# A four-layer graph network on one core: the last sweep over the adjacency matrix with every block split, into nine plus four slots

## The reference

```python
x = _layernorm(x + _L0_gnn_ref(x, adj, W_self, W_neigh))   # adj @ h / deg, deg = clip(row sums of adj, 1)
x = _layernorm(x + _L1_gnn_ref(x, adj, kernel, bias))      # relu(adj @ (x @ K) + bias)
x = _layernorm(x + _L2_gnn_ref(x, adj, W1, b1, W2, b2))    # relu twice: two products with adj
x = _layernorm(x + _L3_gnn_ref(x, adj, W, b))              # x1 = swish(adj @ x @ W + b), x2 = swish(adj @ x1 @ W + b)
```

## Time and profile before

| | |
|---|---|
| median of 3 runs | 1170.21 us (1168.99 to 1171.78) |
| the profiled execution, its own time | 1166.82 us |
| its span, first to last instruction | 1164.6 us |
| PE busy | 1143.0 us, 98% |
| DVE busy | 810.4 us, 70% |
| ACT busy | 539.0 us, 46% |
| granted TensorE clock, mean | 0.996 |
| DMA | 279.45 MB, mean 240 GB/s |

### The profile page before, as it was taken

One profiled execution on the slowest core, in us unless ns is written; L12 is line 12 of the kernel. 1 busy time (PEld: TensorE's weight loads), 2 busy tenths in 40 slices (PEclk: granted clock), 3 DMA queues, 4 the chain that ended last, 5 costly groups with the idle time before them and its releaser, 6 DMA issues.

```text
span 1164.6 us, 13823 instructions
## 1 busy us (share of the span) xinstructions
PE 1143.0 (98%) x4936; PEld 887.7 (76%) x4936; DVE 810.4 (70%) x1091; ACT 539.0 (46%) x612; POOL 69.4 (6%) x48
## 2 busy tenths in 40 slices
PE   7999999999999999999999999999999999999995
PEld 3455767778778888888888888888888888887673
DVE  4888889889898666685545488656496555655883
ACT  1112334444655444474445464544375444544673
POOL 0000000000131111000000010101000000000111
PEclk9999999999999999999999999999999999999998
DMA  8988666655868656496656578566578566756893
GB/s 295 375 290 280 233 226 227 223 203 199 304 238 298 211 192 217 173 339 232 210 189 199 182 268 307 182 216 200 198 276 293 203 204 209 261 219 231 317 337 142
DMA packets 82626, 279.45 MB, mean 240 GB/s; under 512 B 8832, under 2 KB 14208, under 8 KB 82560
## 3 DMA queue, kind: packets, MB, share of 16 engines
q1 hardware_dynamic: 75744, 273.71, 66.9%
q10 hardware_dynamic: 6816, 4.85, 1.4%
HBM read 276.43 MB, written 2.10 MB: 239 GB/s over the span
## 4 chain that ended last, share of the span: by engine, by line
PE 89%; DMA 4%; DVE 3%; ACT 1%; issue 1%; ACTq 1%; POOL 0%; POOLq 0%; DVEq 0%; SPq 0%
PE acc L425 25%; PE acc L420 25%; PE acc L421 25%; PE acc L408 10%; PE acc L457 3%; DMA out<-t_x 2%; DVE adj_lo L685 1%; DMA b<-L_b 1%; DMA raw<-adj_tiles 1%; ACT t_x L526 1%; ACT adj_hi L569 1%; PE acc L443 1%; PE acc L435 1%; DVE stats L600 0%; ACTq L556 0%
## 5 line engine op out<-in xcount | busy, mean ns | idle before, releaser
L685 DVE TENSOR_TENSOR adj_lo<-raw,adj_hi 128x1024 fp32r<-128x1024 f32 x426 | 516.5, 1230 | 210.0 <-ACT adj_hi L569 194.6
L569 ACT CAST adj_hi<-raw 128x1024 fp32r<-128x1024 f32 x426 | 445.2, 1050 | 403.3 <-PE acc L425 243.9
L420 PE MATMUL acc<-adj_hi,op_hi 128*128 128x512 f32 x1352 | 538.4, 398 | 0.0
L421 PE MATMUL acc<-adj_hi,op_lo 128*128 128x512 f32 x1352 | 526.7, 390 | 0.0
L425 PE MATMUL acc<-adj_lo,op_hi 128*128 128x512 f32 x1352 | 417.6, 390 | 1.8 <-DVE adj_lo L685 1.8
L425 PEld LDWEIGHTS acc<-adj_lo,op_hi 128*128 128x128 f32 x1352 | 253.1, 188 | 58.3 <-DVE adj_lo L685 5.4
L420 PEld LDWEIGHTS acc<-adj_hi,op_hi 128*128 128x128 f32 x1352 | 254.1, 188 | 55.2 <-issue 4.3
L421 PEld LDWEIGHTS acc<-adj_hi,op_lo 128*128 128x128 f32 x1352 | 254.1, 188 | 55.0 <-issue 4.3
L589 DVE TENSOR_TENSOR deg_part<-deg_part,raw 128x1024 f32<-128x1024 f32 x120 | 146.6, 1222 | 13.3 <-DMA raw<-adj_tiles 8.3
L408 PE MATMUL acc<-raw,x_rows 128*128 128x512 f32 x312 | 140.7, 600 | 6.8 <-DMA raw<-adj_tiles 6.8
L708 POOL TENSOR_TENSOR rstd<-var_eps,minus_half 128x4 f32<-128x4 f32 x32 | 56.6, 1769 | 1083.2 <-DVE var_eps L605 1083.2
(11 more groups left out here) (45 smaller groups left out, 224.8 us busy)
## 6 DMA issues: line engine op xcount, KB each, us to landing
raw<-adj_tiles SPq DMA_DIRECT2D x518, 512.0 KB, 4.8
x_rows<-x_blocks SPq DMA_DIRECT2D x8, 256.0 KB, 6.2
xt<-x_t ACTq DMA_DIRECT2D x8, 256.0 KB, 5.5
out<-t_x ACTq DMA_DIRECT2D x8, 256.0 KB, 4.2
w<-W ACTq DMA_DIRECT2D x2, 64.0 KB, 8.9
b<-b ACTq DMA_DIRECT2D x2, 64.0 KB, 12.5
w_res<-W_self ACTq DMA_DIRECT2D x1, 64.0 KB, 3.5
w_neigh<-W_neigh ACTq DMA_DIRECT2D x1, 64.0 KB, 4.6
```

The costliest lines, as they stand in the source:

```text
L420: nc.tensor.matmul(bank, op_block(op_hi, p, j), a_hi, start=first and b == 0, stop=False)
L421: nc.tensor.matmul(bank, op_block(op_lo, p, j), a_hi, start=False, stop=False)
L569: nc.scalar.copy(adj_hi[:, s % SPLIT, :], raw[:, g % RAW, :]).then_inc(hi_ready, 1)
L685: nc.vector.tensor_tensor(adj_lo[:, s % SPLIT, :], raw[:, g % RAW, :], adj_hi[:, s % SPLIT, :].bitcast(fp32), ALU.subtract).then_inc(lo_re ...
```

## The change

It does five things.

1. The seven WHOLE blocks of LAST_ORDER become ONE: all 60 steps of the last sweep are split. `kept` and `hidden` go, and the line 408 form with `deg_part`.
2. Four more split slots, numbers 9 to 12, from the load of step 430 on. Slot 9 + i is the quarter i (1024 wide) of `op_hi` and `op_lo` of parity 0, pass 4's operand, from when the last product of pass 4 that reads it is done (COLUMN_END: products 673, 693, 697 and 699).
3. A split step takes the slot whose last reader comes first, instead of slot s % 9. For all steps up to 442 this is the same product to wait for as before. From then on:

| step | waits for product, before | after |
|---|---|---|
| 443 | 674 | 673 |
| 458 | 691 | 690 |
| 459 | 700 | 691 |
| 460 | 701 | 693 |
| 461 | 702 | 697 |
| 462 | (WHOLE) | 699 |
| 463 | (WHOLE) | 700 |
| 464 | 703 | 701 |
| 468 | 707 | 705 |
| 471 | 710 | 708 |
| 512 | 749 | 749 |
| 517 | 754 | 754 |

From 464 on a split may run 13 steps ahead of PE (step g waits for product g + 237).

4. Nearly all entries of the tables move. In passes 0 to 4 most move by one step or one product (WEIGHT_AT by 1, the others by 8 or 16). In the last sweep they move further, as shown:

| chunk m | 40 | 41 | 42 | 43 | 44 | 45 | 46 | 47 |
|---|---|---|---|---|---|---|---|---|
| WEIGHT_AT, before / after | 720/720 | 725/726 | 731/732 | 738/738 | 741/742 | 749/750 | 762/762 | 768/768 |
| SUM_AT, ahead of the split of step | 471/480 | 476/486 | 484/492 | 489/496 | 494/499 | 502/504 | 512/513 | end/end |
| SCALE_AT, ahead of the split of step | 479/489 | 484/494 | 494/498 | 502/502 | 506/505 | 512/end | end/end | end/end |

5. A load waits for the subtraction of the step six before it in all of the last sweep, since no step of it is WHOLE.

```diff
     LAST_ORDER = (
-        [(0, 1, 1, ONE), (0, 2, 1, ONE), (0, 3, 1, WHOLE), (0, 5, 5, ONE), (0, 0, 0, ONE), (0, 5, 6, ONE),
+        [(0, 1, 1, ONE), (0, 2, 1, ONE), (0, 3, 1, ONE), (0, 5, 5, ONE), (0, 0, 0, ONE), (0, 5, 6, ONE),
...
-    KEPT = [CHUNKS - 1 - q for q in (1, 2)]
...
+    COLUMN_END = {k: max(at for at, (g, ahead) in enumerate(PRODUCTS) if STEPS[g][0] + ahead == LAST - 1 and STEPS[g][2] == k)
+                  for k in range(CHUNKS)}
+    SPLIT_SLOT = {}
+    SPLIT_BEFORE = {}
+    slots = [(-1, slot, None) for slot in range(SPLIT)]
+    for s, g in enumerate(SPLIT_STEP):
+        if g == min(step for step in SPLIT_STEP if STEPS[step][0] == LAST):
+            slots += [(max(COLUMN_END[2 * i], COLUMN_END[2 * i + 1]), SPLIT + i, max(COLUMN_END[2 * i], COLUMN_END[2 * i + 1]))
+                      for i in range(4)]
+        until, SPLIT_SLOT[s], SPLIT_BEFORE[s] = min(slots, key=lambda slot: slot[:2])
+        slots.remove((until, SPLIT_SLOT[s], SPLIT_BEFORE[s]))
+        slots.append((LAST_USE[g], SPLIT_SLOT[s], LAST_USE[g]))
...
             def whole_step(at, g, k, h):
                 bank, first, ends = begin(at)
-                if SUM_OF[at][0] == 0:
-                    pe.wait_ge(x_loaded[k], 16)
-                    rows = cols(x_rows, k)
-                else:
-                    pe.wait_ge(op_ready, op_no(LAST, k) + 1)
-                    rows = kept(k)
+                pe.wait_ge(x_loaded[k], 16)
...
+        def split_hi(s):
+            slot = SPLIT_SLOT[s]
+            if slot < SPLIT:
+                return adj_hi[:, slot, :]
+            return op_hi[:, (LAST - 1) % 2, (slot - SPLIT) * TW:(slot - SPLIT + 1) * TW]
...
-                    if s >= SPLIT:
-                        wait_split_used(act, s - SPLIT)
-                    nc.scalar.copy(adj_hi[:, s % SPLIT, :], raw[:, g % RAW, :]).then_inc(hi_ready, 1)
+                    wait_split_free(act, s)
+                    nc.scalar.copy(split_hi(s), raw[:, g % RAW, :]).then_inc(hi_ready, 1)
```

More of the change, by code:

```diff
@@ L329, in rows4, with split_lo @@
             return t.rearrange("p (b d) -> p b d", b=BPC)
-        def kept(k):
-            return deg_part[:, 0, KEPT.index(k) * CW:(KEPT.index(k) + 1) * CW]
-        def hidden(c):
-            return kept(c) if c in KEPT else t_x[:]
+        def split_hi(s):
[3 more added lines that the diff above has]
+            return op_hi[:, (LAST - 1) % 2, (slot - SPLIT) * TW:(slot - SPLIT + 1) * TW]
+        def split_lo(s):
+            slot = SPLIT_SLOT[s]
+            if slot < SPLIT:
+                return adj_lo[:, slot, :]
+            return op_lo[:, (LAST - 1) % 2, (slot - SPLIT) * TW:(slot - SPLIT + 1) * TW]
         def norm_no(m):
@@ L346, in wait_raw, with wait_split_free @@
             eng.wait_ge(raw_loaded[g % RAW], 16 * (g // RAW + 1))
-        def wait_split_used(eng, s):
-            g = SPLIT_STEP[s]
-            if g in EARLY_NO:
-                eng.wait_ge(e_done, EARLY_NO[g] + 1)
-            else:
-                eng.wait_ge(f_done, g + 1)
+        def wait_split_free(eng, s):
+            if SPLIT_BEFORE[s] is not None:
+                g, ahead = PRODUCTS[SPLIT_BEFORE[s]]
+                if ahead:
+                    eng.wait_ge(e_done, EARLY_NO[g] + 1)
+                else:
+                    eng.wait_ge(f_done, g + 1)
         @block.sync
@@ L407, in whole_step @@
                     j = h * BPT + b
-                    last = nc.tensor.matmul(bank, rows[:, j * P:(j + 1) * P], raw[:, g % RAW, b * CW:(b + 1) * CW],
+                    last = nc.tensor.matmul(bank, cols(x_rows, k)[:, j * P:(j + 1) * P], raw[:, g % RAW, b * CW:(b + 1) * CW],
                                             start=first and b == 0, stop=ends and b == BPT - 1)
@@ L424, in split_step @@
                     j = k * BPC + h * BPT + b
-                    last = nc.tensor.matmul(bank, op_block(op_hi, p, j), adj_lo[:, s % SPLIT, b * CW:(b + 1) * CW],
+                    last = nc.tensor.matmul(bank, op_block(op_hi, p, j), split_lo(s)[:, b * CW:(b + 1) * CW],
                                             start=False, stop=ends and b == BPT - 1)
@@ L511, in after @@
                         act.wait_ge(op_ready, m + CHUNKS)
-                    nc.scalar.activation(hidden(c), t_y[:, m % 2, :], ACT.Silu).then_inc(silu_ready, 1)
+                    nc.scalar.activation(t_x[:], t_y[:, m % 2, :], ACT.Silu).then_inc(silu_ready, 1)
                 if p == LAST and u == SILU_AT[m]:
@@ L540, in after @@
                         act.wait_ge(silu_ready, m - 4 * CHUNKS + 1)
-                        nc.scalar.copy(dst, hidden(c)).then_inc(op_hi_ready, 1)
+                        nc.scalar.copy(dst, t_x[:]).then_inc(op_hi_ready, 1)
                 if p == LAST and u == SCALE_AT[m]:
@@ L667, in after @@
                     if p in (0, 4):
[L668 removed]
+                        nc.vector.tensor_tensor(lo, t_x[:], hi, ALU.subtract).then_inc(op_ready, 1)
             for u in range(END * PARTS):
```

46 lines of the change are left out of this document (22 added, 24 removed), and 22 rows, old and new, of tables (BIAS_AT, NORM_AT, SCALE_AT, SUM_AT).

## The result

| | before | after |
|---|---|---|
| median of the runs | 1170.2 us (1168.99 to 1171.78) | 1158.12 us (1157.24 to 1159.29) |
| the profiled execution, its own time | 1166.82 us | 1157.31 us |
| its span | 1164.6 us | 1155.1 us |

The ratio is 0.9895, with an interval of 0.988 to 0.9911. The changed kernel is 12.1 us faster by the medians and 9.5 us by the profiled executions. The prediction had the sign, but 1164.1 us and a range from 1161.0 were too high: it saw 6.1 us of gain.

What follows compares the result with a forecast made beforehand. PE's work and waits were taken as the bound. Terms -4.97 (work), -5.16 (waits), +2.0 (waits back) and +2.05 (tail) sum to -6.1; from the median 1170.2 that forecast 1164.1 us, range 1161 to 1170.5.

Steps and rivals of the forecast that it cites:

- Part 1: Last sweep on PE: fourteen steps split instead of WHOLE, 1.36 us for 1.715 each, giving -4.97 us.
- Part 2: Last sweep, slots and loads: loads run ahead, removing 5.16 us of PE waits, less 2 us that come back.
- dating by hand: Last sweep: event times worked out from profile rows; PE never waits, but four margins are under a microsecond.
- reserve: Last sweep: 2 us of PE waits allowed for slower hand-offs and late stores, range 0 to 5 us.
- better: Last sweep and tail: no waits, and chunk 46's scaling or its store falls into a gap; 1161 to 1162 us, chance 0.10.
- late loads: Last sweep: loads every 1.46 us, sum copies late, PE waits 5 to 9 us; 1167 to 1171, say 1169, chance 0.15.
- lockstep: Last sweep: ACT and DVE wait for each other, 13.5 us per six-step chunk; 12 us slower, 1174 us, chance 0.12.
- Not running ahead: Last sweep: DMA or load slots still hold the loads, saved PE time becomes waits; 1172 us, chance 0.08.
- Part 3: Tail after PE's last work: last scaling waits for chunk 46's store; 14.15 us instead of 12.11, +2.05 us.
- Part 4: Passes 0 to 4: work moves by one step or product, 1.36 to 2.7 us, within 5.6 us of cover; no change.

Runs made afterwards that it cites:

- nine-slot run: Changed kernel without the four extra split slots, its last-sweep tables mostly four steps earlier: 1166.71 us, ratio 0.9977 to the kernel before.
- second pair: Both kernels profiled once more without edits: kernel before 1167.49 us profiled (runs 1168.37), changed kernel 1158.53 us profiled (runs 1158.65, ratio 0.9907).

## Why the prediction was wrong, by its steps

**Part 1 was right.** The work of the last sweep is 87.8 us where it was 92.8; the splits of the fourteen steps cost nothing, for DVE had room (17 of 20 us busy). With 60 products at 1.36 the sweep is down to its nominal work within 0.4 us, and the gain in work is the 4.97 of the rows: the pair of WHOLE products took 3.43 us in the trace, and the 6.4 us of gain would have asked for 3.63.

**Part 2 was right in its mechanism, and its size was off.** The loads run ahead from 1045 us on (291, 297, 360 GB/s), the casts with them, and nothing waits. The dating by hand held. The copies of sums 41 to 44 in ACT's timeline:

```profile
1075.62 0.59 ACT L507 COPY t_agg<-acc 128x512 f32<-128x512 f32 x1 [0.26 <-PE acc L440]
...
1084.95 0.57 ACT L507 COPY t_agg<-acc 128x512 f32<-128x512 f32 x1
...
1093.80 0.59 ACT L507 COPY t_agg<-acc 128x512 f32<-128x512 f32 x1 [0.20 <-PE acc L440]
...
1102.09 0.58 ACT L507 COPY t_agg<-acc 128x512 f32<-128x512 f32 x1
```

They end at 1076.21, 1085.52, 1094.39 and 1102.67. With the 1.63 us by which this execution was early that is 1077.8, 1087.2, 1096.0 and 1104.3, against 1078.0, 1088.1, 1096.1 and 1104.1. The **failed term** of the sum is the one set beside the dating: "2 us of waits, with 0 and 5 as the ends", a reserve for hand-offs and late stores that no row asked for. The waits were 0.38 and 0.26. Where each event is dated from rows and the dates say none, the likeliest value was none. The case called "better" was half true: there were no waits, but the scaling of chunk 46 fell into no gap, and its 1161 to 1162 was still too high. The reserve is only 1.6 of the 6.0 us between 1164.1 and 1158.1; the rest stands under "What is left".

**The late loads did not come**, and the rival had two things wrong. First, it held a load every 1.46 us against PE's 1.36. PE needs a step every 1.36 only up to product 719; from there a multiplication by the weights stands in about every six products, which the prediction itself puts at 9.05 us, 1.51 for a step. From 1060 to 1080 the changed kernel's DMA moved 361 GB/s, which is the rival's rate, and yet the lead was 15.8 us at step 470 and 15.9 at step 490. Second, 359 isn't the most that the loads can bring. The same 20 us of the kernel with the entries of chunks 0 to 39 as before:

```profile
1060.00:1080.00 20.00, 17.29 (x74) 14.21 (x73) 18.13 (x17) 15.92 (x17) 0.00 (x0) 0.91 1.01 403
```

By the Trainium skill (SBUF — State Buffer, "A bandwidth-pool intuition that's wrong", about 358 GB/s to a core) the prediction had the lead lose 2 us in 20 products; in this trace it kept 15 to 18 us up to product 743. The 361 of the changed kernel agrees with that figure, and the 403 lies above it.

**The lockstep** didn't come either, in this kernel. In the nine-slot run ACT and DVE do come late, with 6 us of waits and not 12; that this is the alternation of the two that the rival describes isn't shown. **Not running ahead** can be ruled out by the windows.

**Part 3 was right:** 14.0 us for the forecast 14.15, with the store landing 2.3 us after its issue, as forecast, and the last scaling waiting 2.42 us for it.

**Part 4 was right** in its size. The waits in passes 1 to 4 are the same within half a microsecond, and the run with the entries of chunks 0 to 38 as before is as fast as the changed kernel.

**What is left.** The forecast of the profiled executions was -6.1, and they gave -9.5 and -9.0. Of the 3.4 and 2.9 that are missing, 1.6 to 1.7 are the reserve for waits, 1.6 and 0.4 the start of product 708, and 0.1 to 0.2 the tail; in the second pair the kernel before also waited 0.6 us more. The start of product 708 is luck for the most part: two profiles of one and the same kernel differ in it by 0.1, 1.3 and 2.0 us, in the three kernels profiled twice. The rest of the miss, 2.6 us, is in the base: the median lay 3.4 us above the profiled execution before, and only 0.8 after. The prediction added its difference to the median of three runs, 1170.2; the five other medians of the kernel before were 1168.3 to 1169.4, its 35 timed executions on one chip lie between 1167.1 and 1172.3, and the profiled executions had 1166.8 and 1167.5. So the miss of 6.0 us is made up of 1.6 for the reserve, 0.1 for the tail, 1.6 for the start and 2.6 for the base. With the measured waits in place of the reserve the forecast would have been 1162.5, still outside what came. The range left too little on its lower side: the sum with no waits is 1162.1, and less the 1.4 us by which runs differ 1160.7, above the 1158.1 measured. The timed gain was 10.7 us on a shared chip, 1.5 more than the mean of the profiled ones. Why timed executions of the kernel before lie 0.9 and 3.4 us above its profiled ones, and those of the changed kernel 0.1 and 0.8, no run settles; that stays open.

## What to carry to other kernels

In a queue that works in order, a copy that waits for a distant engine blocks every prefetch behind it: put it where the queue would arrive when it becomes ready, and move it whenever the number of buffers, and so the lead, changes. Here more buffers alone, less work on the busy engine alone, and both without the new order were worth nothing or less, and the whole gained 1%; so date all three as one plan, and if the dates show no wait, forecast none. Hold the rate of the transfers against all that the consumer does in the same stretch, not against its fastest step. And take the base of a forecast from many runs: here it was off by more than the term that failed.
